# Second cross attention: VectorE's preparation of the next batch laid out in single pieces over the steps of the score loop

## What is computed

```
q = _rms_norm(q, q_norm_w); k = _rms_norm(k, k_norm_w)          # q = _layernorm(x), k = v = ctx
q = q * cos + _rotate_half(q) * sin                              # 16 query heads of 32
k = k * cos + _rotate_half(k) * sin                              # 4 key heads of 32
scores = jnp.einsum('bgnqd,bgkd->bgnqk', qg, k) * scale          # causal mask, then softmax
out = jnp.einsum('bgnqk,bgkd->bgnqd', attn, v)
x = x + jnp.tanh(g_xattn[1]) * (out @ w_out.T)
```

## Time and profile before

| | us |
|---|---|
| median of 3 runs | 851.45 (850.57 to 853.03) |
| the profiled execution, its own time | 851.91 |
| its span, first to last instruction | 850.0 |
| PE busy / DVE busy / ACT busy / POOL busy | 661.7 / 643.5 / 610.4 / 385.8 |
| mean granted clock of PE | 0.93 of full speed |

### The profile page before, as it was taken

The page is one execution under the profiler, slowest core; times in us unless marked ns, Lnnn a source line. Parts: engine busy times, 40 slices in busy tenths (PEclk is TensorE's granted clock), DMA queues, the critical chain, the costliest instruction groups (busy, mean ns, idle before and its releaser), DMA issues. The chain is left out here.

```text
span 850.0 us, 13580 instructions
## 1 busy us (share of the span) xinstructions
PE 661.7 (78%) x5134; PEld 355.1 (42%) x5134; DVE 643.5 (76%) x978; ACT 610.4 (72%) x812; POOL 385.8 (45%) x493
## 2 busy tenths in 40 slices
PE   5763277775876756769979897989999887888886
PEld 2431123332432323445654564356545533444443
DVE  1689999999999897886884589456634538888884
ACT  2787699899778994588883697479927226776775
POOL 0116516557595776372472156212303315655552
PEclk9998589799979989689999999999999899999999
DMA  8900220000000000622321021122200010010011
GB/s 313 375 1 0 93 57 1 1 1 1 0 1 2 0 1 0 223 70 69 121 78 34 2 69 35 47 70 76 76 1 2 1 35 1 27 37 26 25 38 50
DMA packets 21760, 43.71 MB, mean 51 GB/s; under 512 B 3904, under 2 KB 8512, under 8 KB 20800
## 3 DMA queue, kind: packets, MB, share of 16 engines
q1 hardware_dynamic: 21696, 42.85, 14.7%
HBM read 38.61 MB, written 4.19 MB: 50 GB/s over the span
## 5 line engine op out<-in xcount | busy, mean ns | idle before, releaser
L1632 DVE TENSOR_REDUCE c_nmax<-c_s 128x1 f32<-128x384 f32 (+3 forms) x176 | 108.5, 633 | 84.2 <-PE c_s L1850 84.1
L1750 ACT ACTIVATE c_probs<-c_e 128x512 f32<-128x512 f32 (+1 forms) x176 | 94.5, 558 | 57.5 <-PE c_e L1880 56.5
L1562 POOL TENSOR_TENSOR c_psum<-c_probs 128x1536 f32<-128x1536 f32 x16 | 55.9, 3493 | 157.2 <-ACT c_probs L1750 157.2
L1333 PE MATMUL b_y<-w2q,b_q2T 128*128 128x512 bf16 x256 | 73.3, 440 | 48.2 <-ACT b_q2T L1250 28.6
L2186 PE MATMUL d_gu<-gateq,d_xqT 128*128 128x512 bf16 (+1 forms) x384 | 83.9, 362 | 17.7 <-ACT d_xqT L2111 15.5
L1847 PE MATMUL c_s<-c_kT,c_qaT 96*128 96x128 f16 (+3 forms) x256 | 72.3, 315 | 21.8 <-DVE c_nmax L1632 20.0
L1304 PE MATMUL b_up<-shared,b_xqT 128*128 128x512 bf16 x256 | 73.2, 412 | 2.4 <-ACT hidden L1216 2.4
L1878 PE MATMUL c_e<-c_qaT,c_kT 98*128 98x512 f16 (+3 forms) x256 | 69.0, 304 | 5.0 <-ACT c_qaT L1737 4.5
L1333 PEld LDWEIGHTS b_y<-w2q,b_q2T 128*128 128x128 bf16 x256 | 26.0, 108 | 86.6 <-issue 43.7
L2186 PEld LDWEIGHTS d_gu<-gateq,d_xqT 128*128 128x128 bf16 x384 | 34.9, 98 | 53.1 <-ACT d_xqT L2111 22.6
L1847 PEld LDWEIGHTS c_s<-c_kT,c_qaT 96*128 96x128 f16 x256 | 25.2, 100 | 69.0 <-DVE c_nmax L1632 41.2
(11 more groups left out here) (237 smaller groups left out, 1854.0 us busy)
## 6 DMA issues: line engine op xcount, KB each, us to landing
c_stage<-in_gateT SPq DMA_DIRECT2D x16, 704.0 KB, 4.0
c_stage<-in_downT SPq DMA_DIRECT2D x6, 768.0 KB, 4.6
xs<-in_x SPq DMA_DIRECT2D x4, 1024.0 KB, 17.7
a_w1f<-in_w1T SPq DMA_DIRECT2D x2, 2048.0 KB, 16.5
hidden<-in_w2T SPq DMA_DIRECT2D x2, 2048.0 KB, 21.1
out<-xs SPq DMA_DIRECT2D x16, 256.0 KB, 2.0
a_ctxT<-in_ctxT SPq DMA_DIRECT2D x1, 1024.0 KB, 5.1
b_ln_g<-in_ln_g SPq DMA_DIRECT2D x1, 1024.0 KB, 4.7
```

What stands on the lines that cost most here:

```text
L1333: last = nc.tensor.matmul(y_ps[:], q2T[:, n % 2, c, :], w2q[:, c, :], start=(c == 0), stop=(c == IC - 1))
L1562: nc.gpsimd.tensor_tensor(psum[:], region(slot, 0)[:, :, P:], region(slot, 1), ALU.add).then_inc(psum_ready, 1)
L1632: nc.vector.tensor_reduce(nmax[:, G % 2, i, n:n + heads], s_ps[u % 2][:, 0:heads * (i + 1) * P].rearrange("p (n k) -> p n k", n=heads), ax ...
L1750: nc.scalar.activation(probs[:, G % 2, at:at + width], e_ps[fill % 3][:, 0:width], ACT.Exp).then_inc(e_read, 1)
```

## The change

Compound pieces are cut in two (`keys_squared` and the new `keys_variance`; `key_parts` and the new `key_rest`; `weighted` and the new `weighted_cos`), and tables give each piece a step of its own. In the first feed forward both halves are called one behind the other, as before. The line numbers of the changed file are 7 to 21 higher in this part.

```diff
+    def keys_variance(self, dve, b):
+        nc = self.nc
+        dve.wait_ge(self.step, self.small.value())
         last = self.small.mark(nc.vector.tensor_reduce(self.kss[:], self.ksq[:], axis=AX, op=ALU.add))
...
+    def key_rest(self, dve, b):
...
         dve.wait_ge(self.khi_ready, b + 1)
         self.nc.vector.tensor_tensor(ka[:, :, 2 * HD:3 * HD], k4, ka[:, :, 0:HD], ALU.subtract).then_inc(self.klo_ready, 1)
...
+    def weighted_cos(self, dve, b, i):
+        nc, n = self.nc, b * TILES + i
         dve.wait_ge(self.xw_ready, n + 1)
...
-        KEYS, KEYS_SCALED, KEYS_TURNED, KEYS_SPLIT = 2, 5, 8, 18
+        KEYS, KEYS_SCALED, KEYS_TURNED, KEYS_SPLIT = 1, 5, 8, 17
         STATS = 9
-        TURN, EACH, SPLIT = 16, 2, 4
+        WEIGHT_AT, COS_AT = (12, 19, 24, 28), (13, 20, 26, 30)
+        TURN_POOL_AT, HEADS_AT, PARTS_AT = (16, 20, 25, 29), (20, 24, 28, 32), (23, 27, 31, 34)
...
                 for i in range(TILES):
-                    if u == TURN + EACH * i:
+                    if u == WEIGHT_AT[i]:
                         prep.weighted(dve, b, i)
-                    if u == TURN + EACH * i + SPLIT:
+                    if u == COS_AT[i]:
+                        prep.weighted_cos(dve, b, i)
+                    if u == PARTS_AT[i]:
                         prep.query_parts(dve, b, i)
```

More of the change, by code:

```diff
@@ L343, in keys_squared @@
             dve.wait_ge(self.khi2_ready, b)
-        last = self.small.mark(nc.vector.tensor_tensor(self.ksq[:], self.kctx[:], self.kctx[:], ALU.mult))
-        dve.wait_ge(self.step, last)
+        self.small.mark(nc.vector.tensor_tensor(self.ksq[:], self.kctx[:], self.kctx[:], ALU.mult))
+    def keys_variance(self, dve, b):
+        nc = self.nc
+        dve.wait_ge(self.step, self.small.value())
         last = self.small.mark(nc.vector.tensor_reduce(self.kss[:], self.ksq[:], axis=AX, op=ALU.add))
@@ L383, in key_parts @@
         self.nc.vector.tensor_copy(ka[:, :, 0:HD], k4).then_inc(self.khi_ready, 1)
+    def key_rest(self, dve, b):
+        k4 = self.ksq[:].rearrange("p t (h j) -> p (t h) j", j=HD)
+        ka = self.kaug[:].rearrange("p t h j -> p (t h) j")
         dve.wait_ge(self.khi_ready, b + 1)
@@ L1116, in _ @@
                     prep.weighted(dve, 0, p - 4)
+                    prep.weighted_cos(dve, 0, p - 4)
                 largest(n + 1)
@@ L1123, in _ @@
                     prep.keys_squared(dve, 0)
+                    prep.keys_variance(dve, 0)
                 if p == 3:
@@ L1131, in _ @@
                     prep.weighted(dve, 0, 3)
+                    prep.weighted_cos(dve, 0, 3)
                 if p == 7:
@@ L1134, in _ @@
                     prep.key_parts(dve, 0)
+                    prep.key_rest(dve, 0)
                     for i in range(TILES):
@@ L1564, in prepare @@
             def prepare(b, u):
-                if u == KEYS:
+                if u == KEYS + 1:
                     prep.keys_scale(pool, b)
@@ L1573, in prepare @@
                 for i in range(TILES):
-                    if u == TURN + EACH * i:
+                    if u == TURN_POOL_AT[i]:
                         prep.turn_queries(pool, b, i)
@@ L1601, in prepare @@
                     prep.keys_squared(dve, b)
+                if u == KEYS + 1:
+                    prep.keys_variance(dve, b)
                 if u == KEYS_SCALED:
@@ L1610, in prepare @@
                     prep.key_parts(dve, b)
+                if u == KEYS_SPLIT + 1:
+                    prep.key_rest(dve, b)
                 for i in range(TILES):
-                    if u == TURN + EACH * i:
+                    if u == WEIGHT_AT[i]:
                         prep.weighted(dve, b, i)
-                    if u == TURN + EACH * i + SPLIT:
+                    if u == COS_AT[i]:
+                        prep.weighted_cos(dve, b, i)
+                    if u == PARTS_AT[i]:
                         prep.query_parts(dve, b, i)
@@ L1794, in _ @@
                     for i in range(TILES):
-                        if u % SPAN == TURN + EACH * i + SPLIT - 1:
+                        if u % SPAN == HEADS_AT[i]:
                             act.wait_ge(tr_done, TURNS_BEFORE(b))
```

## The result

| | before | changed |
|---|---|---|
| median of 6 runs each, us | 851.33 (850.57 to 853.03) | 856.13 (855.49 to 857.52) |
| profiled execution, its span | 850.0 | 854.2 |

The ratio is 1.0054 with a 95% interval of 1.0041 to 1.0066: the change makes the kernel about 0.5% slower, where 0.6% faster was forecast, and the time lies above the range.

What follows compares the result with a forecast made beforehand. PE was taken to idle behind queued DVE pieces in steps 17 to 29, with DVE itself the bound in batch 0. Terms -3.1 - 6.5 - 4.7 + 5.9 + 1.2 + 0.7 + 0.6 = -5.9 gave 846 us, range 838 to 854.5.

Steps and rivals of the forecast that it cites:

- what the change wins: Steps 17 to 29: less PE idle and slow clock, less DVE work in batch 0; -4.7, -3.1, -6.5 us in batches 0 to 2.
- step 13: Clip in batch 2 ends later behind POOL's sum, +1.2 us; cosine race in batch 1 taken as nothing, 1.9 as bound.
- Step 35: PE's transposes wait for tile 3's parts, held at step 34 by POOL's sum: 2.1, 2.1, 1.6 us, +5.9 in the sum.
- slower: Rival, chance 0.15: PE's wait at step 35 also lowers its clock, 2.7 us more per batch; sum +2.3, 854 us.
- The keys' square: At step 1, waiting for the load in batch 0, +0.7 us; held by a sum in batches 1 and 2, +0.3 each.
- Steps 29 to 33 of batch 0: Pieces moved here cost nothing: without projections, DVE comes late to a step 34 that waits for POOL's sum anyhow.
- Hidden after all: Rival, chance 0.15: PE's lead or an earlier sum end hides most of the step 35 wait; 840 us and lower.
- No change: gaps move: Rival, chance 0.20: PE soon waits for busy DVE or ACT in smaller portions; 853 us with half the gains, 851 with two thirds.

Runs made afterwards that it cites:

- Parts3_early: Changed kernel with the last tile's heads back at step 31 and its parts at step 32; 845.09 us, ratio 0.9934 to the kernel before.
- only_parts3: Kernel before with only the last tile's heads moved to step 32 and its parts to step 34; 861.94 us, ratio 1.0106 to the kernel before.
- the repeat: The changed kernel run once more, unaltered, for a second profile; 855.19 us, ratio 1.0039 to the kernel before.
- after_nosum: Changed kernel with POOL's sum of probabilities cut to one column, so results are not the layer's; 834.46 us, ratio 0.9800 to the kernel before.
- tile0_back: Changed kernel with both pieces of tile 0 of the queries back at step 16; 855.66 us, ratio 1.0037 to the kernel before.
- keys_back: Changed kernel with the keys' square back from step 1 to step 2; 854.79 us, ratio 1.0039 to the kernel before.

## Why the prediction was wrong

**What bounds the kernel, and what the change wins: right.** The forecast was -4.7, -3.1 and -6.5 us in steps 17 to 29; measured were -4.5, -3.7 and -6.9, the slow clock of batch 2 included (0.98 for 0.88).

**The failed step is the one on step 13:** "Whether the cosine comes before the sum in batch 1 is close: POOL has two short products left when `xw` ends, DVE one maximum. [...] I take nothing". When `xw` ended, at 426.82, POOL's two products were all but over (426.99): the pair took 1.05 us for 0.60, so `xw` had held it 0.45 us, not 0.6, and no whole product was left. The sum came first by 0.38 us, in both batches and in every kernel with the cosine at step 13. Taken were 0 and 1.2 us; it cost 1.7 and 3.2 in steps 12 to 17. The price that I had named for losing the race, 1.9, was about right for batch 1. For batch 2 I had let the clip alone be held, and not the cosine and the clip one behind the other; PE's clock fell there too, and PE was busy 9.06 us for 7.97 with the same work. A race that I called close should have entered with its price times two batches.

**Step 35: the wait right, its size short.** 2.19, 2.19 and 1.70 us for 2.1, 2.1 and 1.6. But the term was the wait alone. From step 33 to the next batch the changed kernel takes 3.1, 2.2 and 3.0 us longer, 8.3 for my 5.9. The waits alone cost 5.1, and PE's slower clock behind them in batches 0 and 2 another 1.6 each. This was the mechanism of my rival "slower", but at 1.6 us in two batches of three, where I had 2.7 in each. Parts3_early, which returned these 8.3 us to the last tenth, and only_parts3 (8.2) bear the size out.

**The keys' square:** +1.6 in batch 0 (steps 0 to 17) for +0.7, and +0.3 in each of the others, as said. Against five kernels with the square at step 2 the place costs 0.7, as forecast; the other 0.9 stand in those kernels as well, with a later load and a lower clock at the loop's start. The term was right by that comparison, and the excess is scatter. **Steps 29 to 33 of batch 0** cost 0.6 for nothing: no projection covers tile 3 there, PE waits 0.46 us for ACT's exponentials where it did not wait before, and my cover of POOL's sum lies behind these steps.

In the loop the differences from my terms are +3.7 (step 13), +2.4 (35), +0.9 (square), +0.6 (29 to 33) and -0.8 for the gains: from -5.9 to +0.9. The other 3.3 us of the profile lie outside the loop, where the change touches nothing. Of these, 0.7 are scatter of the loop's begin, and 2.6 the hand-over with its slow stretch of the clock, which the repeat has too; what brings it on stays open. The range was too narrow because its costs were bounded one by one, the clock entered the sum only as a gain, and none of these 3 us had a place in it.

**The rivals.** "Hidden after all" is refuted at step 35; the parts of tile 0, which took 2.73 us inside the sum of batch 1 and cost PE 0.81, come nearest to it. "No change: gaps move" comes nearest in the loop, but not for its reason: DVE's load was no limit to the gains, since 15.1 us of them came, and after_nosum keeps them (18.00, 20.35 and 23.27 us in steps 17 to 29). What the Trainium skill states ("SBUF — State Buffer", section "Who interferes with whom"), the exclusive lock on the port pair, agrees with every such piece here: square 2.76, cosine 3.61, parts 2.75, split 3.34, none ending before the sum and each within 0.6 us of its end.

## What to carry to other kernels

A schedule of single short pieces is only as good as its places against the long instructions of the other engine on the shared port: here 15 us of gains came out as 0.5% slower or 1.0% faster, by where three pieces stood, and 1.4% faster with one wait more. Count for each moved piece what the other engine holds at that time, and ask first whether someone waits for that piece itself; a lead of two steps hides a held maximum partly, and a held input of the next step not at all. A one-sided order (the long instruction waits for the short one) cost POOL 0.39 us at that place and removed a race that cost the loop 3. And do not read a total alone: here the loop's begin, one load and one slow stretch of PE's clock moved a profile by 1 to 3 us each beside the edit under test, and only the stretches of the timeline told them from it.

## What was not expected of the hardware

An instruction of 0.18 us takes 3.34 when POOL's sum starts 0.11 us ahead of it, and PE stands idle 3.08 us for it. How early POOL's sum starts was itself set by the pieces that had been moved out of its way: in the kernel before the sum of that group began at 533.30, behind the split at 525.82, and in tile0_back it begins just ahead of it. POOL is not behind any more, and meets what it never met before.

The same wait of PE at step 35 was followed by the slower clock in some batches and not in others: after 2.19 us it came in batch 0 of the changed kernel and not in batch 1, and in keys_back in batch 1 and not in batch 0. With it the steps to the next batch took 1.6 us more.
